# Masks, a popcount and a lookup placed elsewhere, and zero matmuls in TensorE's stream, in a one-core graph kernel

## The reference

```
adj_d  = adjacency with every skip-th neighbour removed
vals   = where(adj_d > 0, x[neighbour], inf)
s      = sort(vals, over the neighbours)          # per node and feature
agg    = 0.25 * quantile(s, 0.25) + 0.5 * quantile(s, 0.5) + 0.25 * quantile(s, 0.75)
y      = relu((x + agg) @ W1 + b1) @ W2 + b2
x      = layernorm(x + y * mask)
```

## Time and profile before

| | |
|---|---|
| profiled execution | 3872.41 us, its span 3870.6 us, mean granted TensorE clock 0.811 |
| three runs | 3866.15 us median, 3860.3 to 3867.21 |
| busy in the span | VectorE 3180.9 us (82%), TensorE 2635.5 (68%), weight loads 1215.1 (31%), ScalarE 1949.1 (50%), GpSimd 8.0 |
| stages of the span | up to about 510 us sorting, then 16 graphs up to about 3560 us, then blocks 3 and 4 |

### The profile page before, as it was taken

How to read it: one execution, slowest core, us unless ns; L and a number is a source line. 1 busy time by engine, 2 the same in 40 slices (tenths; PEclk the granted TensorE clock), 3 DMA queues, 4 the chain that set the end, 5 groups by cost and what they waited for, 6 DMA issues and landing times. The chain is left out here.

```text
span 3870.6 us, 48616 instructions
## 1 busy us (share of the span) xinstructions
PE 2635.5 (68%) x16944; PEld 1215.1 (31%) x17098; DVE 3180.9 (82%) x5858; ACT 1949.1 (50%) x2672; POOL 8.0 (0%) x21
## 2 busy tenths in 40 slices
PE   0000155777777877778777778787878787887897
PEld 0000022333333333333333333333323333333665
DVE  8999988888888888787878787878888887855676
ACT  2114444565656565656565646565656565553232
POOL 0000000000000000000000000000000000000000
PEclk6555576898889888888898989888989898887777
DMA  1001001323232323222232323232322222332111
GB/s 36 0 14 46 0 11 22 57 40 56 35 57 37 55 38 56 37 54 39 52 42 50 50 41 57 33 59 35 56 43 48 45 49 44 40 56 39 44 33 33
DMA packets 242849, 158.50 MB, mean 41 GB/s; under 512 B 126504, under 2 KB 228026, under 8 KB 242362
## 3 DMA queue, kind: packets, MB, share of 16 engines
q1 hardware_dynamic: 238490, 154.49, 23.8%
q10 hardware_dynamic: 4128, 1.05, 0.2%
HBM read 40.14 MB, written 14.70 MB: 14 GB/s over the span
## 5 line engine op out<-in xcount | busy, mean ns | idle before, releaser
L1002 ACT ACTIVATE hot<-bcast,consts 128x1024 bf16<-128x1024 f32 x744 | 829.8, 1115 | 487.4 <-PE bcast L567 486.8
L1386 DVE SCALAR_TENSOR_TENSOR prod<-near,consts,rows 128x512 f32<-128x512 bf16 x768 | 566.5, 746 | 323.1 <-PE rows L580 219.5
L580 PE MATMUL rows<-hot,table 128*64 128x512 bf16 x4608 | 729.6, 428 | 115.0 <-DVE prod L1386 103.8
L554 PE MATMUL ring<-member,neigh_t 128*128 128x512 bf16 x1924 | 516.3, 407 | 179.4 <-ACT words L963 149.1
L589 PE MATMUL found_bank<-prod,consts 128*64 128x512 f32 x1536 | 446.3, 656 | 3.9 <-DVE prod L1386 3.9
L567 PE MATMUL bcast<-idx_t,consts 32*128 32x512 f16 x1488 | 315.4, 421 | 171.6 <-ACT hot L1002 158.3
L580 PEld LDWEIGHTS rows<-hot,table 128*64 128x64 bf16 x4608 | 225.9, 116 | 408.8 <-issue 320.4
L554 PEld LDWEIGHTS ring<-member,neigh_t 128*128 128x128 bf16 x2048 | 182.6, 103 | 527.7 <-ACT words L963 193.6
L492 PE MATMUL ring<-identb,adj_b 128*128 128x128 bf16 x256 | 35.6, 272 | 380.1 <-ACT adj_b L890 367.5
L567 PEld LDWEIGHTS bcast<-idx_t,consts 32*128 32x128 f16 x1488 | 71.0, 92 | 540.3 <-ACT hot L1002 364.6
L963 ACT ACTIVATE words<-ring 128x512 uint16<-128x512 f32 x256 | 146.5, 592 | 146.8 <-PE ring L554 146.0
(11 more groups left out here) (332 smaller groups left out, 4371.5 us busy)
## 6 DMA issues: line engine op xcount, KB each, us to landing
near<-idx_bt SPq DMA_DIRECT2D x768, 128.0 KB
late<-in_adj_dram SPq DMA_DIRECT2D x16, 1024.0 KB, 5.6
adjt_d<-late SPq DMA_DIRECT2D x16, 512.0 KB, 2.8
adj_l<-adjt_d SPq DMA_DIRECT2D x16, 512.0 KB, 5.6
adj_s<-adjt_d SPq DMA_DIRECT2D x16, 512.0 KB, 3.5
parts_d<-parts SPq DMA_DIRECT2D x6, 512.0 KB, 5.1
table<-parts_d SPq DMA_DIRECT2D x192, 16.0 KB, 2.2
out_dram<-x_all SPq DMA_DIRECT2D x4, 512.0 KB, 3.8
```

The costliest lines, as they stand in the source:

```text
L554: ins = mm(ring[u % 2][:, :], kept_t[:, j, P * i:P * i + P], member[:, j, n // 2, 512 * (n % 2):512 * (n % 2) + 512], start=(j == 0), stop ...
L580: ins = mm(rows[u % 2][C * h:C * h + C, :], table[:, s, GROUPS * h + g8, :], hot[:, u % HOT, h, :], start=(s == 0), stop=(s == 2))
L1002: run(hot[:, u % HOT].rearrange(flat), spread_bank(l, u)[0][:, 0:2, :].rearrange(flat), ACT.Relu, bias=eq_bias[:, :]).then_inc(S["hot_read ...
L1386: stt(out=prod[:, u % DEEP, :], in0=near[:, u % NEAR, :], scalar=iota_b[:, :], in1=rows[u % 2][:, :], op0=ALU.is_equal, op1=ALU.mult).then ...
```

## The change

On ScalarE the three masks of tile 0 are made at the end of the region before (behind the last chunk of tile 0, before `keep_sum`), and those of tile 1 one at a time between the chunks of tile 1; the hot evictions of units 3 to 5 there stand in other places too. On TensorE lookup 2 (`units(l, 3)`) stands between chunks 4 and 5 in place of behind the two sums. On VectorE the second popcount stands behind `gcn_start`. Two helpers multiply zeros of 128 x 512 bf16: `run_free` into dense_bank while nothing uses it, `run_on` into found_bank, where the zeros are added to the sums. There are 22 of the first and 50 of the second in a graph. The index transposes get a wait for the dense part's last read of dense_bank (gcn_ev). GpSimd sets the zeros once. The three masks of tile 0 of graph 0 are made ahead of its select.

```diff
--- before.py
+++ after.py
@@ build
+        zeros = sb("zeros", [P, 512], BF16)
@@ gpsimd
+            made(g.memset(zeros[:, :], 0.0))
@@ tensor
+            def run_on(l, n):
+
+                for _ in range(n if l is not None else 0):
+                    mm(found_bank[:, :], zeros[:, 0:P], zeros[:, :], start=False, stop=False, skip_group_check=True)
+
+            def run_free(n):
+
+                for _ in range(n):
+                    mm(dense_bank[:, :], zeros[:, 0:P], zeros[:, :], start=True, stop=True)
+
             def select(b, l):
 
                 if l is not None:
+                    run_free(4)
                     spread(l, 0)
+                    run_free(3)
                     spread(l, 1)
+                    run_free(3)
                     units(l, 2)
+                    run_free(12)
                 if not b:
                     for n in range(4):
                         chunk(b, 1, n)
                 chunk(b, 1, 4)
+                units(l, 3)
                 chunk(b, 1, 5)
                 sum_first(b, 0)
                 sum_size(b, 0)
-                units(l, 3)
                 chunk(b, 1, 6)
@@
                     for s in range(10):
+                        if i == 2 and s == 4:
+                            run_on(l, 6)
                         if i + 1 < NT and s < CW:
                             chunk(b, i + 1, s)
@@ region
                     turn_adj(p, 0, 2)
+                    run_on(l, 5)
                 units(l, STEP[3] + 1)
                 if p is not None:
                     turn_adj(p, 2, NT)
+                    run_on(l, 5)
                 units(l, STEP[5])
+                run_on(l, 8)
                 if p is not None:
                     count_neighbours(p)
+                    run_on(l, 8)
                 if d is not None:
                     dense_turn(d)
@@
                     count_up(p, 3)
+                run_on(l, 10)
                 units(l, STEP[8])
@@
                     count_kept(p)
+                run_on(l, 8)
                 units(l, STEP[13])
@@
                 if t is not None:
+                    wait(pe, S["gcn_ev"], 0 if d is None else d + 1)
                     turn_idx(t)
@@ scalar, select
                 units(l, 3)
-                for i in range(2):
-                    for k in range(TAUS):
-                        mask(b, i, k)
                 chunk(b, 1, 2)
                 chunk(b, 1, 3)
+                mask(b, 1, 0)
+                units(l, 4)
                 chunk(b, 1, 4)
-                units(l, 4)
+                units(l, 5)
                 chunk(b, 1, 5)
+                mask(b, 1, 1)
                 keep_sums(b, 0)
                 chunk(b, 1, 6)
-                units(l, 5)
+                units(l, 6)
                 chunk(b, 1, 7)
-                units(l, 6)
+                mask(b, 1, 2)
@@ scalar, region
+                    for k in range(TAUS):
+                        mask(p, 0, k)
                 if l is not None:
                     keep_sum(l, d)
@@ vector, region
                     clear_own(p)
-                if t_of is not None:
-                    pop(wl, x2, x4, x8, t)
                 units(l, STEP[5])
                 if d is not None:
                     gcn_start(d)
+                if t_of is not None:
+                    pop(wl, x2, x4, x8, t)
                 if p is not None:
                     members(p, 1)
```

More of the change, by code:

```diff
@@ L1129, in _ @@
                     tag(0, 0)
+            for k in range(TAUS):
+                mask(0, 0, k)
             for b in range(B):
```

## The result

The changed kernel takes **3799.9 us** (median of four runs, 3798.4 to 3801.7) against 3866.7 (also of four) for the kernel before: ratio 0.983, 95% interval 0.981 to 0.985. That is 67 us faster where 96 were forecast.

A forecast was written before the change was run, and what follows sets the result against it. VectorE was taken as the bound, with 31.6 us of each 187.73 us period not its work. Masks, tile 2, popcount and loop ends summed to 96 us off 3866, giving 3770 us, range 3735 to 3835.

The forecast's parts named there:

- the sum: Whole kernel: 15 x 3.4 + 15 x 1.45 + 14 x 1.8 + 1 - 3 = 96 us gained.
- L1434's idle time: VectorE's size product: its idle time on ScalarE's masks falls from 134.6 to under 40 us.
- the share of low clock: TensorE over a period: the low clock takes under 15% of the time in place of 24%.
- the waits for values 0, 2 and 3: VectorE at the start of select: waits for looked-up rows of about 8 us.
- the period of 181 us: Graph loop: one period falls from 187.73 us to near 181 us.
- the transpose: Dense transpose on TensorE: comes some 2 us earlier relative to ffn_end, the wait after it gone.
- Masks: Start of select: earlier masks cut VectorE's 9.2 us wait to about 1.5; gain 3.4 us a graph, bounds -0.5 to 4.3.
- Tile 2: Before chunk (3,4): six zeros fill a TensorE gap and keep the clock up; gain 1.45 us a graph, bounds 0 to 1.7.
- Popcount and neighbour count: Around the dense transpose: earlier norm, with 5 + 8 + 8 zeros, removes a 1.82 us wait; gain 1.8 us, 14 graphs.
- The ten zeros: Before units 37: cost nothing, as ScalarE reaches the spread's operand 3.0 us later than TensorE asks.
- The fourth: Whole kernel slower: zeros don't raise the clock and delay TensorE, chiefly at the dense transpose; 3909 us, chance 0.09.
- The second rival: Start of select: low clock from the new gap, cold lookups replace the mask wait; masks gain 0.3, 3817 us, chance 0.18.

The follow-up runs named there:

- the popcount back: The changed kernel with the second popcount again ahead of the dense norm on VectorE; 3846.1 us, one of four executions at 3797.5.
- the nine zeros: Changed kernel with middles ahead of the popcount, without twelve zeros behind lookup 1; four before first spread removed, nine added before chunk 2 of tile 1; 3720.2 us.
- the masks alone: Against the kernel before, only the masks and lookup 2 moved; popcount in its old place, no zeros; 3785.2 us.

## Why the prediction was right or wrong

The sign, the range and the main cause were right; the time was 30 us too low, a third of the forecast gain. That it was no more is in part luck: in the profiled executions a period fell by 3.8 us where the sum has 6.65, which over fourteen periods is 53 us in place of 93, but the two ends of the loop brought about 20 us where the sum has 3. The range itself is wider than its working: 15 x 1.5 us is 22 either way of 3770, and 3740 to 3805 were written. Of the signs, L1434's idle time, the share of low clock (a mean of 0.94 is 12% of the time) and the waits for values 0, 2 and 3 (7.4 us for about 8) came as said, the period of 181 us did not, and the transpose came 3.5 us earlier against ffn_end and not 2. Step by step:

**Masks.** Right in mechanism: the masks ended well before VectorE asked, the index transposes were next in line, about 2.5 us late, and the twelve zeros lay on the path. 3.4 us were forecast with the clock low up to the third spread; in the traced period it stayed up and the gain was 4.6, a little over the upper bound of 4.3. The choice of the lower clock rested on the gap of 2.3 us; a low stretch does follow that gap, but not in every course of the loop. It does in nearly all periods with the popcount back, where the eight chunk matmuls behind the gap take 3.31 us in place of 1.90, and in two of thirteen of the changed kernel, where the size product then waits 3.07 and 2.95 us. The twelve were priced at 2.7 us; in this tile they cost 1.7, because TensorE would have waited 0.83 of it for ScalarE, and 1.3 a graph over the whole kernel.

**Tile 2.** 1.4 us for 1.45. Right here, but only beside the other zeros: by themselves the six shift the low stretch.

**Popcount and neighbour count.** This is the step that failed. The wait of 1.82 us went as forecast, and the step then said that the gain "can't be more, as VectorE is then continuously busy". It did not ask what TensorE meets next once it is early. TensorE met the second count, whose release (`middles`) stayed where it was on VectorE, behind the popcount and the members, so it came no earlier with it. Idle time of 0.54 us became 5.05, the clock fell behind it, and 4.0 us a graph came back, 56 of the 96 us of the sum over the 14 graphs with a dense part. Zeros in the idle time took back 2.35 of the 4.0; releasing the count earlier took back 3.3 (4.65 to 1.37). A step that lets one engine run ahead has to be followed to that engine's next wait on the other; the prediction did this on VectorE and not on TensorE.

**The ten zeros** before units 37 were put at nothing and cost 0.24 us (a wait at the lookup value at 1496.29 that the kernel without zeros doesn't have); the other covered ones showed nothing.

**The rivals.** The fourth (zeros don't raise the clock) is refuted: runs of zeros stand at 0.22 us each with the granted clock at 1.00, and in the kernel with the popcount back the clock rises within the twelve (3.7 us for what takes 5.2 at one level and 2.6 at the other). The Trainium skill ("TensorE: Matmul & The Clock Gate", Part 1: The HAM clock gate) says that the clock follows how busy the array has been; the runs agree, for all-zero operands too. The same page's Part 4 sets transposes apart in this; in the changed kernel the clock stays at 1.00 through 7.1 us of which 4.7 are transposes, against what the page says. With the popcount back it falls while the last of them run (0.54 from 1371 on), so whether they play a part there stays open. The second rival (cold row path) didn't come about in the changed kernel, but is what the kernel with the popcount back does.

**Left open:** what decides in which of its two courses that kernel runs; how much of the zeros around the neighbour count is needed, as single groups were not tried apart from the six and the twelve; and what the nine zeros bring without the four being taken away.

## What to carry to other kernels

When a wait is removed, follow both engines to their next meeting: the one that now comes early may idle there, and on TensorE idle time is paid a second time in the clock of the work behind it. Zero matmuls pay inside a gap that exists in the changed kernel and cost where it has been closed: sixteen in a gap of 5.05 us brought 43 us, twelve where only 0.83 us would have been idle cost 19. Releasing the count earlier brought the same 43 us without any. A part of a change should be timed without the others; here the masks alone were worth more than the whole. And one period of a trace is not the kernel: the periods beside it have to be looked at before a wait is called typical.

## What the runs showed of the hardware

The value of an edit depended on where low-clock stretches fell, and these move when anything in the loop moves: taking the popcount's move out of the changed kernel left TensorE's order as it was, and yet the waits at the start of select went from 8.6 to 14.5 us. Zeros keep the granted clock up as other matmuls do: 0.22 us each at 1.00, and with them no low stretch at the first lookups where without them there is one of 6.8 to 10.2 us in every period. One kernel had executions at 3846.1 to 3846.3 and at 3797.5 us, a spread of 1.3% where the others stay within about 0.35%, and periods of 187.7 and of 184 us in one and the same trace.
